# Two tiles of the slots' second MLP product made together on TensorE, the last quarter of both at the end

## The chip, the core and the metric

The kernel runs on one core of a Trainium2 chip. A core has TensorE (matrix products, PE in the profile, its weight loads PEld), VectorE (DVE), ScalarE (ACT), GpSimd (POOL) and SyncE (SP, which issues DMAs). They run side by side and wait for each other through semaphores. TensorE writes its sums into PSUM, eight banks of 128x512 fp32 numbers; ScalarE and VectorE read them there. The metric is the device time of one execution in microseconds (us), as the median of several runs. Lower is better.

## What is computed

The reference has a slot-attention block and, behind it, a routed transformer block. The change touches the first. For each of 4 samples there are 1024 keys and values and 1024 "slots" of 512 numbers, and three rounds (T = 3) refine the slots:

```python
slots = q_mu + jnp.exp(q_logsig) * noise
for _ in range(T):
    prev = slots
    q = _ln(slots, lnq_g, lnq_b) @ wq + bq
    logits = jnp.einsum('bnd,bkd->bnk', k, q) / scale
    attn = jax.nn.softmax(logits, axis=-1) + EPS_ATTN
    attn = attn / jnp.sum(attn, axis=1, keepdims=True)
    upd = jnp.einsum('bnk,bnd->bkd', attn, v)
    slots = upd @ wu + bu + prev
    h = _ln(slots, lnm_g, lnm_b) @ w1 + b1
    slots = jax.nn.gelu(h, approximate=False) @ w2 + b2 + slots
    slots = _ln(slots + x_cls[:, None, :], lnp_g, lnp_b)
```

The product with `w2` in the line before the last is the second MLP product. `w1` and `w2` are 512x512.

## The kernel before

**Tiles.** The 1024 slots of a sample are eight tiles of 128 rows, numbered 0 to 7 here as j in the code. Twelve calls of `slot_round` follow each other (4 samples, 3 rounds each). I number the calls 1 to 12 (g = 0 to 11). Calls 3, 6, 9 and 12 are the last rounds of their samples; 3, 6 and 9 prepare the next sample's slots, and call 12 leads over to the routed block. The other eight calls (1, 2, 4, 5, 7, 8, 10, 11) have one and the same order of work at the place of the change and are called the eight plain rounds.

**Precision.** Each factor is held as a high and a low half (names ending in h and l), and `mm3` (lines 219 to 221) makes one product out of three matmuls: low by high, high by low, high by high. A product over 512 rows of contraction has four quarters (C = 4), so 12 matmuls of 128x512 into one bank.

**The MLP.** `hidden(h, f)` makes quarter f of the hidden layer for half h of the slots (tiles 0 to 3 or 4 to 7) in a bank. ScalarE reads it twice as GELU (lines 1930 and 1931, into `gbuf` and the high half `gT1h`), and GpSimd subtracts the two for the low half `gT1l` (`split_gelu`, line 2619), which adds one to the semaphore `g_split`. `down(j)` multiplies tile j's columns of the four quarters with `w2` into bank `DB[j]` = (2, 3, 4, 5, 4, 5, 0, 1)[j]. So `down(4)` and `down(5)` use banks 4 and 5 again, after tiles 2 and 3; they first wait for `down_read`, which says that VectorE has read the earlier tile from the bank. Before each quarter, `down` waits for that quarter's `g_split`. At its end it adds one to `down_done`.

**VectorE behind it.** The order on each engine is fixed by hand. For each tile VectorE runs `residual(j)`: wait for `down_done`, add the bank to `slots` into `tbuf` (line 2379), and take mean and variance of it (lines 1994 and 1996); then `gained(j)` (line 2386), and, after GpSimd has made the reciprocal deviation `rs_p` (lines 2517 and 2519), `new_slots(j)` (line 2392) with the statistics of the next round's norm. ScalarE normalizes the tile (line 1744), TensorE transposes it (`z_transpose`, line 1496), ScalarE takes the transpose's high half (`zTh`, line 1762) and VectorE its low half (`z_lo(yn, j)`, line 2042, `zTl`). In a plain round VectorE's order from tile 3's new slots on is: `new_slots(3)`, `z_lo` 0 and 1, `residual(4)`, `gained(4)`, `residual(5)`, `new_slots(4)`, `gained(5)`, `z_lo` 2 and 3, `residual(6)`, `new_slots(5)`, `gained(6)`, `residual(7)`, `new_slots(6)`, `gained(7)`, `z_lo` 4, `new_slots(7)`, and, in the next call, `z_lo` 5, 6 and 7.

**TensorE around it.** Its order is `hidden(1, 0)` to `hidden(1, 3)`, transposes 0 and 1, `down(4)`, `down(5)`, transpose 2, `down(6)`, transpose 3, `down(7)`. The next call opens with `logits(0, 0)` (keys by the first four tiles of slots; waits for `z_lo` 3), transpose 4, `logits(1, 0)`, transpose 5, `logits(2, 0)`, and then `logits_pair(0, 2)`, matmuls of 128x256 that use tiles 4 and 5 and so wait for `z_lo` 5. In call 12 the place of the transposes is taken by two transposes of the routed block, `T(0, 0)` and `T(0, 1)`.

Of the kernel before, what the change touches and what calls it, by code (L numbers as in the profile page):

```python
# [5 lines left out]
C = D // P  # L6
# [13 lines left out]
AHEAD = 4  # L20
# [21 lines left out]
def build(nc, a):  # L42
# [3 lines left out]
    def sem(name):  # L46
        if name not in sems:
            sems[name] = nc.alloc_semaphore(name)
        return sems[name]

    def at(name, shape, off, dt=f32):
        return nc.alloc_sbuf_tensor_at(name, shape, dt, offset=BASE + off)

    def scratch(name, shape, dt=f32):
# [14 lines left out]
    w2 = [at("w2h", [P, C, D], 16 * KB, f32r), at("w2l", [P, C, D], 24 * KB, f32r)]  # L69
# [6 lines left out]
    gT = [[at(f"gT{h}h", [P, C, 512], OP + 16 * KB * h, f32r),  # L76
           at(f"gT{h}l", [P, C, 512], OP + 16 * KB * h + 8 * KB, f32r)] for h in range(2)]
# [136 lines left out]
    def bank(i):  # L214
        return ps[:, i, :]

    def mm3(pe, out, lhs, rhs, start, stop):
        (lh, ll), (rh, rl) = lhs, rhs
        nc.tensor.matmul(out, ll, rh, start=start, stop=False)  # L219
        nc.tensor.matmul(out, lh, rl, start=False, stop=False)  # L220
        return nc.tensor.matmul(out, lh, rh, start=False, stop=stop)  # L221

    def pair(t, *ix):
        return t[0][ix], t[1][ix]

    ALL = slice(None)

    def cut(j, n=P):
        return slice(j * n, (j + 1) * n)
# [1053 lines left out]
    with block:  # L1283
# [190 lines left out]
        def _(pe):  # L1474
# [31 lines left out]
            def z_transpose(yc, j):  # L1506
                pe.wait_ge(sem("zo_z"), yc + j + 1)
                if j >= 2:
                    pe.wait_ge(sem("lo_z"), yc + j - 1)
                transposes(zbuf[:, j % 2, :], 6 + j % 2).then_inc(sem("tr_z"), 1)  # L1510
# [86 lines left out]
            def slot_round(g, last):  # L1597
                n8 = g * NT
# [89 lines left out]
                DB = (2, 3, 4, 5, 4, 5, 0, 1)  # L1688

                def down(j):  # L1690
                    h = j // 4
                    if j in (4, 5):
                        pe.wait_ge(sem("down_read"), AHEAD + n8 + j - 1)
                    for f in range(C):
                        pe.wait_ge(sem("g_split"), g * 2 * C + h * C + f + 1)
                        last_ = mm3(pe, bank(DB[j]), pair(gT[h], ALL, f, cut(j % 4)), pair(w2, ALL, f, ALL),
                                    f == 0, f == C - 1)
                    last_.then_inc(sem("down_done"), 1)

                yn = yc + NT  # L1700
                if t == 0 and b:
# [11 lines left out]
                if g == 0:  # L1713
                    pe.wait_ge(sem("w_split"), 2)
                down(0); down(1); m_transpose(7); down(2); down(3)
                hidden(1, 0); hidden(1, 1); hidden(1, 2); hidden(1, 3)
                if not last:
                    z_transpose(yn, 0); z_transpose(yn, 1)
                down(4); down(5)
                if last:  # L1720
                    T(0, 0); T(0, 1)
                if not last:
                    z_transpose(yn, 2)
                down(6)
                if not last:
                    z_transpose(yn, 3)
                down(7)

            for g in range(B * ROUNDS):
                slot_round(g, g == B * ROUNDS - 1)  # L1730
# [1040 lines left out]
```

## Time and profile before

| | us |
|---|---|
| median of 3 runs | 2335.23 (2334.9 to 2336.6) |
| the profiled execution | 2333.35 |
| its span on the core, first to last instruction | 2331.6 |
| TensorE busy | 2293.4 (98% of the span) |
| VectorE busy | 1571.5 (67%) |
| ScalarE busy | 976.1 (42%) |
| GpSimd busy | 990.0 (42%) |

Between the profiled execution and its span lie 1.75 us, and the profiled execution is 1.9 us under the median. The matmuls of TensorE are pipelined: one that reads 0.39 us long is followed by the next 0.23 us after its start. So a gap in the stream can be longer than the idle time that the profile gives, and starts are compared here, not busy times. The chain that ended last runs through TensorE for 79% of the span, VectorE for 11% and GpSimd for 5%. Each round takes about 142 us.

### The profile page before, as it was taken

To read this page: it belongs to the slowest core of one execution; us is meant where nothing else is said; L and a number is where in the kernel's file an instruction comes from. 1 tells how busy PE (TensorE), PEld (TensorE's weight loads), DVE (VectorE), ACT (ScalarE), POOL (GpSimd) and SP (SyncE) were. 2 spreads that over 40 slices of the span, in tenths; PEclk is the share of its full clock that TensorE was granted. 3 is DMA by queue.
4 is the path that set the end of the run, shared out by engine and by line. 5 is a ranking of instruction groups with operands and counts; after the bars stand their busy time and mean duration, and the time that the engine had idled before them with its cause. 6 is when DMAs were issued, how large, how long until landed. Compare 5 with 4: busy or idle time off the path is not lost.

```text
span 2331.6 us, 30994 instructions
## 1 busy us (share of the span) xinstructions
PE 2293.4 (98%) x11509; PEld 1885.6 (81%) x11509; DVE 1571.5 (67%) x3069; ACT 976.1 (42%) x1650; POOL 990.0 (42%) x1345
## 2 busy tenths in 40 slices
PE   8999999999999999999999999999999999899998
PEld 4888888888888888888888888888888887777886
DVE  6778557757477574778757667785675868764642
ACT  2566443343333334333333433334333335766332
POOL 1576235152453525435454352464535246753200
PEclk9999999999999999999999999999999999999999
DMA  5587000000052000013400002250000012204330
GB/s 204 179 315 278 1 1 1 1 1 1 37 199 86 1 24 5 14 51 127 154 5 14 14 5 59 109 172 5 10 14 5 19 46 91 69 33 145 96 113 19
DMA packets 87126, 158.59 MB, mean 68 GB/s; under 512 B 10801, under 2 KB 33337, under 8 KB 83134
## 3 DMA queue, kind: packets, MB, share of 16 engines
q1 hardware_dynamic: 82838, 150.26, 18.8%
q0 software_dynamic: 2688, 6.31, 0.9%
q8 instruction: 92, 1.51, 0.3%
q14 instruction: 58, 0.48, 0.1%
q10 hardware_dynamic: 1450, 0.04, 0.0%
HBM read 106.21 MB, written 50.37 MB: 67 GB/s over the span
## 4 chain that ended last, share of the span: by engine, by line
PE 79%; DVE 11%; POOL 5%; issue 2%; ACT 2%; DMA 1%; ACTq 0%; SPq 0%; DVEq 0%; POOLq 0%
PE ps L219 25%; PE ps L221 24%; PE ps L220 24%; PE ps L1496 3%; DVE moments L1994 3%; POOL gT1l L2619 2%; DVE slots L2392 1%; DVE zTl L2042 1%; DVE tbuf L2379 1%; DVE tbuf L2386 1%; PE ps L1649 1%; DVE mx L2339 1%; ACT prob L1897 1%; PE ps L1481 1%; PE ps L447 1%
## 5 line engine op out<-in xcount | busy, mean ns | idle before, releaser
L219 PE MATMUL ps<-zTh,kTl 128*128 128x512 f32 (+1 forms) x912 | 332.2, 364 | 2.8 <-ACT prob L1897 2.2
L221 PE MATMUL ps<-zTh,kTh 128*128 128x512 f32 (+1 forms) x912 | 324.6, 356 | 0.0
L220 PE MATMUL ps<-zTl,kTh 128*128 128x512 f32 (+1 forms) x912 | 324.4, 356 | 0.0
L219 PE MATMUL ps<-vh,prob_lo 128*128 128x512 f32 x768 | 306.1, 399 | 0.0
L221 PE MATMUL ps<-vh,prob_hi 128*128 128x512 f32 x768 | 300.1, 391 | 0.0
L220 PE MATMUL ps<-vl,prob_hi 128*128 128x512 f32 x768 | 299.4, 390 | 0.0
L2517 POOL TENSOR_SCALAR rs_m<-mv_m 128x1 f32<-128x1 f32 x96 | 55.3, 576 | 542.3 <-DVE mv_m L1996 540.6
L2042 DVE TENSOR_TENSOR zTl<-ps,zTh 128x512 fp32r<-128x512 f32 x224 | 151.1, 682 | 193.0 <-ACT zTh L1762 193.0
L1897 ACT ACTIVATE prob<-ps,nb 128x1024 f32<-128x1024 f32 x96 | 107.2, 1117 | 252.7 <-DVE nb L2344 252.2
L1744 ACT ACTIVATE zbuf<-slots,rs_m 128x512 f32<-128x512 f32 x96 | 78.4, 817 | 303.3 <-POOL rs_m L2522 303.3
L219 PEld LDWEIGHTS ps<-zTh,kTl 128*128 128x128 f32 x912 | 172.0, 189 | 35.0 <-DVE zTl L2042 7.0
L221 PEld LDWEIGHTS ps<-zTh,kTh 128*128 128x128 f32 x912 | 172.0, 189 | 24.9
L220 PEld LDWEIGHTS ps<-zTl,kTh 128*128 128x128 f32 x912 | 172.3, 189 | 23.5
L1762 ACT ACTIVATE zTh<-ps 128x512 fp32r<-128x512 f32 x224 | 130.6, 589 | 143.7 <-PE ps L1496 143.6
L2361 DVE SCALAR_TENSOR_TENSOR slots<-ps,rcol,slots 128x512 f32<-128x512 f32 x96 | 72.0, 750 | 148.6 <-PE ps L221 147.8
L221 PEld LDWEIGHTS ps<-vh,prob_hi 128*128 128x128 f32 x768 | 144.1, 188 | 31.3
L220 PEld LDWEIGHTS ps<-vl,prob_hi 128*128 128x128 f32 x768 | 144.5, 188 | 28.2
L219 PEld LDWEIGHTS ps<-vh,prob_lo 128*128 128x128 f32 x768 | 144.4, 188 | 28.0 <-issue 0.2
L1867 ACT ACTIVATE prob_hi<-prob 128x1024 fp32r<-128x1024 f32 (+2 forms) x120 | 103.8, 884 | 126.3 <-PE ps L221 101.9
L219 PE MATMUL ps<-zTh,w1l 128*128 128x512 f32 x384 | 150.7, 392 | 0.0
L221 PE MATMUL ps<-zTh,w1h 128*128 128x512 f32 x384 | 149.7, 390 | 0.0
L220 PE MATMUL ps<-zTl,w1h 128*128 128x512 f32 x384 | 149.4, 389 | 0.0
(328 smaller groups left out, 5652.2 us busy)
## 6 DMA issues: line engine op xcount, KB each, us to landing
ctx<-in_ctx_dram SPq DMA_DIRECT2D x8, 1024.0 KB, 7.6
slots<-in_x_dram SPq DMA_DIRECT2D x8, 1024.0 KB, 6.6
kT_d<-kTh SPq DMA_DIRECT2D x6, 1024.0 KB, 8.0
kT_d<-kTl SPq DMA_DIRECT2D x6, 1024.0 KB, 10.6
s_d<-slots SPq DMA_DIRECT2D x6, 1024.0 KB, 5.1
v_d<-vh SPq DMA_DIRECT2D x6, 1024.0 KB, 8.9
v_d<-vl SPq DMA_DIRECT2D x6, 1024.0 KB, 11.7
kTh<-kT_d SPq DMA_DIRECT2D x3, 2048.0 KB, 10.5
```

Of the source, the lines that this page charges most:

```text
L219: nc.tensor.matmul(out, ll, rh, start=start, stop=False)
L220: nc.tensor.matmul(out, lh, rl, start=False, stop=False)
L221: return nc.tensor.matmul(out, lh, rh, start=False, stop=stop)
L1496: last = nc.tensor.transpose(bank(dst_bank)[:, cut(c)], src[:, cut(c)], ident[:, :])
L1744: return A.activation(out, src, ACT.Identity, bias=rs[k][:, j, 1:2], scale=rs[k][:, j, 0:1])
L1762: A.activation(zT[0][:, :, cut(col)], bank(6 + j % 2).rearrange("p (c n) -> p c n", c=C), ACT.Copy)\
L1867: A.activation(prob_hi[:, j % 2, ix, :], prob[:, j // 4, ix, cut(j % 4)], ACT.Copy)\
L1897: A.activation(prob[:, :, i, :], ps[:, b0:b0 + 2, :], ACT.Exp, bias=nb[:, i:i + 1], scale=LOGIT_SCALE, accum_out=esum[:, i:i + 1]).then_in ...
L1994: V.bn_stats(st[k][:, s, :], src).then_inc(sem(f"mv_{k}"), 1)
L2042: V.tensor_tensor(zT[1][:, :, cut(col)], bank(6 + j % 2).rearrange("p (c n) -> p c n", c=C), zT[0][:, :, cut(col)].bitcast(f32), ALU.subtr ...
L2361: V.scalar_tensor_tensor(slots[:, j, :], bank(j % 6), rcol[:, j:j + 1], slots[:, j, :], ALU.mult, ALU.add).then_inc(sem("upd_read"), 1)
L2517: G.tensor_scalar(rs[k][:, j, 1:2], mv[k][:, j, 1:2], LN_EPS, None, ALU.add).then_inc(sem(f"nm_{k}"), 1)
```

## The change

`down` keeps its form for six tiles. Tiles 4 and 5 are made by a new helper, `down_two(4)`, which writes the first three quarters of tile 4, then the first three of tile 5, then the last quarter of tile 4 and the last of tile 5. Each quarter's matmuls are now in `down_part(j, f)`, with the wait for `g_split` in front and the step of `down_done` behind the fourth. The wait for `down_read` stays in front of each tile's first quarter. No matmul is added or taken away, and the banks and all other engines' orders stay the same.

```diff
                     for f in range(C):
-                        pe.wait_ge(sem("g_split"), g * 2 * C + h * C + f + 1)
-                        last_ = mm3(pe, bank(DB[j]), pair(gT[h], ALL, f, cut(j % 4)), pair(w2, ALL, f, ALL),
-                                    f == 0, f == C - 1)
-                    last_.then_inc(sem("down_done"), 1)
+                        down_part(j, f)
+
+                def down_part(j, f):
+                    h = j // 4
+                    pe.wait_ge(sem("g_split"), g * 2 * C + h * C + f + 1)
+                    last_ = mm3(pe, bank(DB[j]), pair(gT[h], ALL, f, cut(j % 4)), pair(w2, ALL, f, ALL),
+                                f == 0, f == C - 1)
+                    if f == C - 1:
+                        last_.then_inc(sem("down_done"), 1)
+
+                def down_two(j):
+
+                    for k in range(2):
+                        pe.wait_ge(sem("down_read"), AHEAD + n8 + j + k - 1)
+                        for f in range(C - 1):
+                            down_part(j + k, f)
+                    down_part(j, C - 1); down_part(j + 1, C - 1)
...
-                down(4); down(5)
+                down_two(4)
```

TensorE, call 1, from the third quarter of `down(4)` on, before. The rows do not name the bank. The wait for `down_read` opens tile 5; the three matmuls ahead of it are tile 4's last quarter.

```order
L219 MATMUL ps<-w2h_51,gT1l_64 128x512 [waits g_split]
L220 MATMUL ps<-w2l_52,gT1h_63 128x512
L221 MATMUL ps<-w2h_51,gT1h_63 128x512
L219 MATMUL ps<-w2h_51,gT1l_64 128x512 [waits g_split]
L220 MATMUL ps<-w2l_52,gT1h_63 128x512
L221 MATMUL ps<-w2h_51,gT1h_63 128x512
L219 MATMUL ps<-w2h_51,gT1l_64 128x512 [waits g_split,down_read]
L220 MATMUL ps<-w2l_52,gT1h_63 128x512
L221 MATMUL ps<-w2h_51,gT1h_63 128x512
```

The same place after the change, from the same third quarter on. Tile 5 now opens directly behind it.

```order
L219 MATMUL ps<-w2h_51,gT1l_64 128x512 [waits g_split]
L220 MATMUL ps<-w2l_52,gT1h_63 128x512
L221 MATMUL ps<-w2h_51,gT1h_63 128x512
L219 MATMUL ps<-w2h_51,gT1l_64 128x512 [waits g_split,down_read]
L220 MATMUL ps<-w2l_52,gT1h_63 128x512
L221 MATMUL ps<-w2h_51,gT1h_63 128x512
L219 MATMUL ps<-w2h_51,gT1l_64 128x512 [waits g_split]
L220 MATMUL ps<-w2l_52,gT1h_63 128x512
```

Nine matmuls of tile 5 now stand between tile 4's third quarter and its last.

VectorE, call 1, `residual(4)`, `gained(4)`, `residual(5)` and `new_slots(4)`; this order is the same before and after.

```order
L2379 TENSOR_TENSOR tbuf_71<-ps,slots_66 128x512 [waits down_done,slots_ready,cb_added]
L1994 BN_STATS moments_88<-tbuf_71 128x6 [waits down_read]
L1996 BN_AGGR mv_p_92<-moments_88 128x2 [waits mv_p]
L2386 SCALAR_TENSOR_TENSOR tbuf_71<-tbuf_71,mv_p_92,gp_row_67 128x512 [waits mv_p]
L2379 TENSOR_TENSOR tbuf_71<-ps,slots_66 128x512 [waits down_done,slots_ready,cb_added]
L1994 BN_STATS moments_88<-tbuf_71 128x6 [waits down_read]
L1996 BN_AGGR mv_p_92<-moments_88 128x2 [waits mv_p]
L2392 SCALAR_TENSOR_TENSOR slots_66<-tbuf_71,rs_p_99,bp_row_68 128x512 [waits nm_p,gp_step]
```

The first row waits for tile 4's `down_done`, and the three behind it have to run before the fifth row, which waits for tile 5's.

## Rows read from the trace of the kernel before

**Rows 1.** Waits of the whole span: us in total, times, longest.

```profile
PE ps L219 <- POOL gT1l L2619: 2.5, 11, 0.7
DVE tbuf L2379 <- PE ps L221: 11.3, 16, 1.1
```

**Rows 2.** Timeline, PE, call 1, `down(4)` and `down(5)`: start, duration, instruction [idle before].

```profile
382.50 0.39 PE L221 MATMUL ps<-w2h,gT1h 128*128 128x512 f32 x1
383.07 0.50 PE L219 MATMUL ps<-w2h,gT1l 128*128 128x512 f32 x1 [0.19 <-POOL gT1l L2619]
...
383.64 0.39 PE L221 MATMUL ps<-w2h,gT1h 128*128 128x512 f32 x1
...
386.38 0.40 PE L221 MATMUL ps<-w2h,gT1h 128*128 128x512 f32 x1
```

**Rows 3.** Timeline, DVE, call 1, from `residual(4)` to `z_lo` 5.

```profile
384.17 0.69 DVE L2379 TENSOR_TENSOR tbuf<-ps,slots 128x512 f32<-128x512 f32 x1 [1.10 <-PE ps L221]
...
385.84 0.78 DVE L2386 SCALAR_TENSOR_TENSOR tbuf<-tbuf,mv_p,gp_row 128x512 f32<-128x512 f32 x1
386.91 0.69 DVE L2379 TENSOR_TENSOR tbuf<-ps,slots 128x512 f32<-128x512 f32 x1 [0.29 <-PE ps L221]
...
390.69 1.28 DVE L2042 TENSOR_TENSOR zTl<-ps,zTh 128x512 fp32r<-128x512 f32 x2
...
395.03 0.72 DVE L2386 SCALAR_TENSOR_TENSOR tbuf<-tbuf,mv_p,gp_row 128x512 f32<-128x512 f32 x1
395.66 0.68 DVE L2379 TENSOR_TENSOR tbuf<-ps,slots 128x512 f32<-128x512 f32 x1
...
401.65 0.66 DVE L2042 TENSOR_TENSOR zTl<-ps,zTh 128x512 fp32r<-128x512 f32 x1
```

**Rows 4.** Busy time by stretch: us, busy of PE, PEld, DVE, ACT, POOL, granted clock, DMA.

```profile
386.91:402.31 15.40, 15.39 (x75) 12.39 (x73) 14.91 (x28) 4.73 (x7) 8.86 (x18) 1.00 0.00 0
1940.00:1947.00 7.00, 6.32 (x29) 4.89 (x28) 4.34 (x6) 4.01 (x7) 5.80 (x10) 1.00 0.55 184
1968.00:1972.00 4.00, 4.00 (x26) 3.33 (x26) 3.20 (x12) 1.91 (x10) 1.55 (x5) 0.57 0.00 0
```

**Rows 5.** Timeline, PE, opening of call 2: `logits(0, 0)`, and `logits_pair(0, 2)`.

```profile
393.01 0.39 PE L219 MATMUL ps<-zTh,kTl 128*128 128x512 f32 x1
...
401.92 0.39 PE L221 MATMUL ps<-zTh,kTh 128*128 128x512 f32 x1
402.36 0.39 PE L219 MATMUL ps<-zTh,kTl 128*128 128x256 f32 x1
```

**Rows 6.** Timeline, PE, call 3, around `down(4)`'s last quarter.

```profile
666.39 0.39 PE L221 MATMUL ps<-w2h,gT1h 128*128 128x512 f32 x1
...
667.19 0.40 PE L220 MATMUL ps<-w2l,gT1h 128*128 128x512 f32 x1
```

**Rows 7.** Timeline, DVE, call 3: `residual(4)` and `z_lo` 2.

```profile
669.36 0.68 DVE L2379 TENSOR_TENSOR tbuf<-ps,slots 128x512 f32<-128x512 f32 x1
...
671.66 0.69 DVE L2042 TENSOR_TENSOR zTl<-ps,zTh 128x512 fp32r<-128x512 f32 x1 [0.67 <-ACT zTh L1762]
```

**Rows 8.** Timeline, DVE, call 6: `residual(4)` and `z_lo` 3.

```profile
1096.56 0.68 DVE L2379 TENSOR_TENSOR tbuf<-ps,slots 128x512 f32<-128x512 f32 x1
...
1101.85 0.66 DVE L2042 TENSOR_TENSOR zTl<-ps,zTh 128x512 fp32r<-128x512 f32 x1
```

**Rows 9.** Timeline, PE, call 6's end: third quarter of `down(4)`, later `logits(0, 0)`.

```profile
1091.81 0.39 PE L221 MATMUL ps<-w2h,gT1h 128*128 128x512 f32 x1
...
1102.56 0.50 PE L219 MATMUL ps<-zTh,kTl 128*128 128x512 f32 x1
```

**Rows 10.** Timeline, PE, call 12: `down(4)`, and the first scores behind the rounds.

```profile
1943.29 0.39 PE L221 MATMUL ps<-w2h,gT1h 128*128 128x512 f32 x1
1944.36 0.50 PE L219 MATMUL ps<-w2h,gT1l 128*128 128x512 f32 x1 [0.69 <-POOL gT1l L2619]
...
1967.71 0.50 PE L434 MATMUL ps<-qk 32*128 32x128 f32 x4 [2.21 <-DVE nmax L907]
```

## The prediction
> **What bounds the kernel now.** I read the chain that ended last first: TensorE has 79% of it and is busy for 98% of the span. So a stop in TensorE's stream counts in full unless the stream stops again later for something that did not move. The view of waits names the stop that the change is about: TensorE waits 11 times for GpSimd's `gT1l`, the low half of the GELU, 2.5 us in all. The same view holds a second row that matters more: VectorE waits 16 times for TensorE before line 2379, 11.3 us in all [rows 1]. Sixteen is two in each of the eight plain rounds, `residual(4)` and `residual(5)`, as the timeline of VectorE shows with 1.10 and 0.29 us [rows 3]. So VectorE takes tile 4 as soon as TensorE has it.
>
> Then the timeline, engine by engine, from `down(4)` to the next call's `logits_pair(0, 2)`. VectorE is busy for 14.91 of the 15.40 us from `residual(5)` to the end of `z_lo` 5 [rows 4], and `z_lo` 5 ends at 401.65 + 0.66 = 402.31. TensorE's last full matmul starts at 401.92 and the next should follow 0.23 later, at 402.15. It starts at 402.36, 0.05 behind the end of `z_lo` 5 [rows 5]. So over the tail of each plain round the two engines are level, and VectorE is the later one by 0.2 us. That decides the case.
>
> **What the change takes away.** The stream's step is (386.38 - 383.64) / 12 = 0.228 us [rows 2]. From the last matmul of the third quarter (382.50) to the last of the fourth (383.64) lie three matmuls, 0.68 us of work in 1.14, so the stop costs 0.46 us. With nine matmuls of tile 5 in between (9 x 0.228 = 2.05 us), the fourth quarter is asked for at 384.78 instead of 382.73. GpSimd has it by 383.07, where TensorE now starts, so 1.7 us of cover are left. The stop goes in all eight plain rounds, and the new wait for `down_read` at tile 5 finds tile 3 read long before. At the end of `down(5)` TensorE is 0.46 us ahead of today.
>
> **What the change puts off.** Tile 4's last matmul starts at 382.50 + 12 x 0.228 = 385.24 instead of 383.64. `residual(4)` starts 0.53 us behind that start (384.17 - 383.64), so at 385.77: 1.60 us later. Tile 5's last matmul comes at 385.92, so tile 5 is free to be read at 386.45. But VectorE must do tile 4 first. From `residual(4)` to `gained(4)` it takes 385.84 - 384.17 = 1.67 us without a wait. The instruction behind a `gained` can start 0.63 us (395.66 - 395.03, a short one of 0.72) to 0.78 us (the whole length of this one) after it [rows 3]. So `residual(5)` starts at 388.07 to 388.22, against 386.91: 1.16 to 1.31 us later. I take 1.2, as back-to-back rows overlap like the short one.
>
> **What hides the delay: nothing.** Behind `residual(5)` VectorE has no wait for TensorE up to `z_lo` 5, it is in arrears there. GpSimd's reciprocals follow VectorE's means and move with them. ScalarE is busy for 4.73 of the 15.40 us [rows 4]. On the way `z_lo` 3 ends at 390.69 + 1.28 + 1.2 = 393.17, while TensorE, 0.46 early, wants `logits(0, 0)` at 393.01 - 0.46 = 392.55 [rows 3, 5]. It stops there for 0.6 us, which eats the gain on the spot and leaves TensorE some 0.2 to 0.3 us behind today. The second stop is at `logits_pair(0, 2)`: `z_lo` 5 ends at 403.51 and TensorE goes on at 403.56 instead of 402.36, **1.2 us later in every plain round**. What follows (transposes 6 and 7, the softmax) starts from TensorE and VectorE at this point, so it all moves along. Eight rounds give 8 x 1.2 = +9.6 us.
>
> **The other four calls.** Call 3: the fourth quarter's first two starts show a stop of 667.19 - 666.39 - 2 x 0.228 = 0.34 us [rows 6]. `residual(4)` would start at 666.39 + 12 x 0.228 + 0.53 = 669.66 instead of 669.36, and the 0.67 us that VectorE idles ahead of `z_lo` 2 for ScalarE and TensorE take that up [rows 7]. The gain stays: -0.34. Call 6 (9 is alike): tile 4 would be ready at 1091.81 + 2.74 + 0.53 = 1095.08, before VectorE comes to it at 1096.56, so nothing is put off. But TensorE waits at `logits(0, 0)`, which starts at 1102.56, for `z_lo` 3, which ends at 1101.85 + 0.66 = 1102.51 [rows 8, 9]. Arriving earlier only makes that wait longer: 0. Call 12: a stop of 1.07 - 0.23 = 0.84 us and the restart goes [rows 10], VectorE does not wait for tile 4 there (it is none of the 16), and the next thing TensorE waits for is VectorE again, 2.21 us for `nmax`: 0.
>
> **The sum.** 9.6 - 0.34 = +9.3 us. On the profiled execution, 2333.35 us, that is 2342.6; on the median, 2335.23, it is 2344.5. The bounds of the unknown pieces: 1.16 to 1.31 per plain round give 9.3 to 10.5; up to 0.4 us of gain in each of calls 6 and 9 and 0.9 in call 12, if their waits give way, take 1.7 off. Own range of the forecast: 2342.5 to 2345.4, and with 1 us for the median's scatter 2341.5 to 2346.5.
>
> **A rule weighed.** Tile 4 is read and worked on from 384.17 to 386.62 while tile 5's matmuls run to 386.38 [rows 2, 3]; after the change that overlap is all but gone. The Trainium skill, "Perfetto Trace Analysis", Optimizing Tensor Performance, has it that independent groups of matmuls should rotate through the banks so that the reading of one overlaps the next group's matmuls. This change speaks against that; by that rule the sum is what I have. The same page, Optimization Strategy, would have one find the gaps on the engine to be filled and take away what blocks them, which by itself gives the sum of the first rival.
>
> **Rivals.**
> - **The tail has room, the gain stays.** If the delay of tile 4 is absorbed, the plain rounds give -0.46 each: -3.7, with call 3 -4.0, so 2331.2. For it: VectorE is busy for only 67% of the whole span. Against it: 14.91 of 15.40 us in the tail, and no wait in it to take up more than 0.2. It decides once `z_lo` 5 has 1.2 us to spare; it has less than nothing. If the calls 6, 9 and 12 gave their part too (0.4 + 0.4 + 0.9), 2329.5. Not slower, 0.08; faster by over 0.2% only in the second form, 0.03 of these.
> - **Half of it is absorbed.** VectorE's start times hang on small gaps and on its sharing with GpSimd (the two `gained` shown take 0.72 and 0.78 us). If such pieces give back 0.6 us a round: 8 x 0.6 - 0.3 = +4.5, 2339.7. The gaps in the tail add up to 15.40 - 14.91 = 0.49 us, and most are the distance between two dependent instructions. 0.10.
> - **The new stop lowers TensorE's clock.** The stop at `logits_pair(0, 2)` is about 1.1 us, after one of 0.6. In this trace, after the 2.21 us wait in call 12 the granted clock reads 0.57 over 4 us: most of it at the lower level, 1.2 of 2.4 GHz, 0.43 x 4 = 1.7 us of work lost. After the gap of 1.07 us there it stays at 1.00 [rows 4, 10]. The new stops are like the second. If the clock fell in every plain round: 8 x (1.2 + 1.7) - 0.3 = +22.9, 2358. The Trainium skill, "TensorE: Matmul & The Clock Gate", A second HAM failure mode, tells of a kernel whose short idles between groups brought the clock down again and again; the trace disagrees so far, as its eleven short stops leave the clock alone. 0.04.
> - **The wait moves but the stop stays.** If GpSimd's fourth quarter came later than 2.05 us after it is now asked for, the stop would remain. The longest today is 1.07 us, in call 12. It is under 0.01.
>
> **How the numbers follow.** Forecast 0.78, half absorbed 0.10, all absorbed 0.08, clock 0.04. The likeliest gives 2344.5. The range runs from 2338.5, which takes in the half-absorbed case, to 2347.5. 0.2%, about what a measurement of this kernel can tell from no change, is 4.7 us: under 2330.5 is faster, over 2339.9 slower. Faster 0.03. Same 0.13: the rest of the absorbed case and most of the half-absorbed. Slower 0.84.
>
> **What would show it.** In the changed kernel's timeline, call 1: no stop in `down(4)`; `residual(4)` 1.6 us later, its wait for TensorE 2.7 instead of 1.10 us; no wait before `residual(5)`; and the view of waits with 8 waits before line 2379 where there were 16. A wait of TensorE for `zTl` at `logits(0, 0)` in the plain rounds, and one of about 1.1 us at `logits_pair(0, 2)`. Each plain round, about 142 us now, gets 1.2 us longer. I am wrong if plain rounds get shorter, if VectorE shows a wait between `residual(5)` and `z_lo` 5, or if the granted clock is under 1.00 in the tails.

## The result

| | before | changed |
|---|---|---|
| median, us | 2335.07 (6 runs, 2334.63 to 2336.6) | 2343.72 (6 runs, 2342.12 to 2345.11) |
| span of the profiled execution, us | 2331.6 | 2341.1 |
| TensorE busy, us | 2293.4 | 2293.8 |
| VectorE busy, us | 1571.5 | 1570.1 |

The ratio of the changed kernel to the one before is 1.0036, with a 95% interval of 1.0026 to 1.0047: it is slower by 8.65 us, where 9.3 was forecast. The work is the same, as the busy times show. What grew is waiting. Of the executions behind the experiments below, one of the kernel before and one with two quarters ahead ran at a mean granted clock of 0.65 and 0.56 and took 3274 and 3836 us; the ratios leave both out, and without its one the median with two quarters ahead is 2338.27 us.

The stop that the change was made against is gone: the view of waits of the changed kernel has no row of TensorE for `gT1l` any more, which stood there with 2.5 us [rows 1]. In its place stands a wait of TensorE for VectorE, and VectorE's wait ahead of its first read of the bank (now line 2392, all lines below the change are 13 higher) has gone from 16 times and 11.3 us to this:

```profile
DVE tbuf L2392 <- PE ps L221: 21.6, 9, 2.7
PE ps L219 <- DVE zTl L2055: 12.4, 18, 0.9
```

The columns are us in total, times and the longest. Nine is one in each plain round and one in call 3. TensorE waits 18 times, two in each plain round and one in each of calls 6 and 9. Now VectorE's timeline in call 1, which answers to [rows 3]:

```profile
385.72 0.69 DVE L2392 TENSOR_TENSOR tbuf<-ps,slots 128x512 f32<-128x512 f32 x1 [2.67 <-PE ps L221]
386.45 0.69 DVE L2007 BATCH_NORM_STATS2 moments<-tbuf 128x6 f32<-128x512 f32 x1
387.18 0.18 DVE L2009 BATCH_NORM_AGGREGATE mv_p<-moments 128x2 f32<-128x6 f32 x1
387.39 0.78 DVE L2399 SCALAR_TENSOR_TENSOR tbuf<-tbuf,mv_p,gp_row 128x512 f32<-128x512 f32 x1
388.09 0.68 DVE L2392 TENSOR_TENSOR tbuf<-ps,slots 128x512 f32<-128x512 f32 x1
...
391.87 1.28 DVE L2055 TENSOR_TENSOR zTl<-ps,zTh 128x512 fp32r<-128x512 f32 x2
...
402.82 0.66 DVE L2055 TENSOR_TENSOR zTl<-ps,zTh 128x512 fp32r<-128x512 f32 x1
```

The first row is `residual(4)`: it waits 2.67 us instead of 1.10 and starts 1.55 later. The row at 388.09 is `residual(5)`, 1.18 us later than 386.91, and it has no wait: tile 5 has been ready for some time, and VectorE is still at tile 4. `z_lo` 5 in the last row is 1.17 us later than 401.65. In between nothing was made up. TensorE at the opening of call 2, which answers to [rows 5]:

```profile
393.20 0.50 PE L219 MATMUL ps<-zTh,kTl 128*128 128x512 f32 x1 [0.53 <-DVE zTl L2055]
...
403.54 0.39 PE L219 MATMUL ps<-zTh,kTl 128*128 128x256 f32 x1 [0.91 <-DVE zTl L2055]
```

These are the two new stops, at `logits(0, 0)` and at `logits_pair(0, 2)`. The second starts 1.18 us later than 402.36. The view of busy time by stretch, over the same 15.40 us of VectorE's work as [rows 4], from `residual(5)` on:

```profile
388.09:403.49 15.40, 14.02 (x67) 10.90 (x65) 14.91 (x29) 4.13 (x6) 9.23 (x18) 1.00 0.00 0
```

VectorE is busy for the same 14.91 us, and TensorE for 14.02 where it was 15.39.

A round's length can be read without the scatter of whole runs, as the distance between the first row maxima of two calls (`mx`, line 2339 before, 2352 after). In the changed kernel the first rows of calls 2 and 3 are

```profile
410.69 1.23 DVE L2352 TENSOR_REDUCE mx<-ps 128x1 f32<-128x1024 f32 x1 [1.79 <-PE ps L221]
553.80 1.23 DVE L2352 TENSOR_REDUCE mx<-ps 128x1 f32<-128x1024 f32 x1 [1.79 <-PE ps L221]
```

so the distance in which call 2's tail lies is 143.11 us; before they stand at 409.51 and 551.47, 141.96 us. The table has these lengths, named by the call whose tail lies in them, for all kernels of this study:

| kernel | plain rounds, us (8) | call 3 | calls 6, 9 |
|---|---|---|---|
| before | 141.93 to 142.02 | 141.49 | 142.26, 142.27 |
| changed | 143.11 to 143.19 | 141.15 | 142.27, 142.27 |
| one quarter ahead | 141.75 to 141.79 | 141.15 | 142.27, 142.30 |
| two quarters ahead | 142.45 to 142.56 | 141.14 | 142.30, 142.28 |
| signal held back | 143.00 to 143.41 | 141.53 | 142.30, 142.30 |
| last rounds only | 141.94 to 142.10 | 141.14 | 142.30, 142.28 |
| changed, `z_lo` 5 early | 142.05 to 142.11 | 141.17 | 142.28, 142.31 |
| before, `z_lo` 5 early | 141.61 to 141.79 | 141.53 | 142.29, 142.30 |
| one quarter, `z_lo` 5 early | 141.14 to 141.16 | 141.15 | 142.30, 142.28 |

Changed less before over the eleven distances is 9.1 us.

### The profile page after: what moved, and what is told of

The parts are those of the page before. It is cut to its first block, busy times and chain, and to the rows that moved or that the text cites. A ratio compares the mean times of both kernels' runs of the same rounds, so it can differ in the third digit from the quotient of the medians.

```text
span 2341.1 us, 30994 instructions
## 1 busy us (share of the span) xinstructions
PE 2293.8 (98%) x11509; PEld 1887.1 (81%) x11509; DVE 1570.1 (67%) x3069; ACT 976.2 (42%) x1650; POOL 989.7 (42%) x1345
## 4 chain that ended last, share of the span: by engine, by line
PE 83%; DVE 11%; POOL 2%; issue 2%; ACT 2%; DMA 0%; ACTq 0%; DVEq 0%; POOLq 0%
PE ps L219 26%; PE ps L221 25%; PE ps L220 25%; PE ps L1496 3%; DVE moments L2007 3%; DVE slots L2405 1%; DVE tbuf L2392 1%; DVE zTl L2055 1%; DVE tbuf L2399 1%; PE ps L1649 1%; PE ps L447 1%; ACT prob L1910 1%; PE ps L1481 1%; DVE mx L2352 1%; PE ps L434 0%
```

## The experiments

My theory: the loss is VectorE's. The change hands it tile 4 later than it takes tile 5 sooner, and VectorE has no room up to the value that TensorE waits for. The rival theories: the split of the sums and the turning between two banks cost TensorE time by themselves; or the new stop at `logits(0, 0)` is what costs. None of the seven kernels leaves work out.

**How many quarters of tile 5 go ahead.** In two kernels `down_two` got a number, 1 or 2, where the change has 3.

```diff
-                    for k in range(2):
-                        pe.wait_ge(sem("down_read"), AHEAD + n8 + j + k - 1)
-                        for f in range(C - 1):
-                            down_part(j + k, f)
-                    down_part(j, C - 1); down_part(j + 1, C - 1)
+                    pe.wait_ge(sem("down_read"), AHEAD + n8 + j - 1)
+                    for f in range(C - 1):
+                        down_part(j, f)
+                    pe.wait_ge(sem("down_read"), AHEAD + n8 + j)
+                    for f in range(ahead):
+                        down_part(j + 1, f)
+                    down_part(j, C - 1)
+                    for f in range(ahead, C):
+                        down_part(j + 1, f)
```

One quarter:

> The same output as before. Only one quarter of tile 5 (three matmuls, 0.68 us) is put between tile 4's third quarter and its last. VectorE's tail theory: the stop of 0.46 us goes, since the last quarter is asked for at 382.73 + 0.68 = 383.41, behind 383.07. Tile 4 is ready 0.23 us later than before the change, so residual(5) starts at 384.40 + 2.37 = 386.77 against 386.91, and logits_pair(0, 2) of the next call 0.14 us earlier. Eight plain rounds: -1.1 us, call 3: -0.34, together -1.5 us, about 2333.6. Theory that the split itself or the turning between two banks costs TensorE 1.2 us a round: the time stays near that of the change, +9 us. Theory that TensorE's stop at logits(0, 0) is what costs: no such stop here, so -4 us, the whole stop gained.

Measured: 2333.34 us against 2335.64, ratio 0.9996 (0.9987 to 1.0005), not to be told from no change by the whole runs. The rounds are clearer: 141.77 us on average, 0.19 less than before, against 0.14 expected; with call 3 that is 8 x 0.19 + 0.34 = 1.9 us. The stop has gone as in the change, though the sums are split and the banks take turns as there, so neither costs anything. What TensorE won is spent at `logits_pair(0, 2)` (timeline of TensorE):

```profile
402.18 0.39 PE L221 MATMUL ps<-zTh,kTh 128*128 128x512 f32 x1
402.93 0.38 PE L219 MATMUL ps<-zTh,kTl 128*128 128x256 f32 x1 [0.36 <-DVE zTl L2059]
```

The distance of 0.75 us should be 0.23. There is no stop at `logits(0, 0)` here, and still TensorE got back only 0.19 of 0.46 us. So that stop is not what takes the gain here.

Two quarters:

> The same output as before. Two quarters of tile 5 are put between tile 4's third quarter and its last. VectorE's tail theory: tile 4 is read 0.91 us later than before the change, residual(5) at 385.08 + 2.37 = 387.45, 0.54 us later, and so is logits_pair(0, 2). Eight plain rounds +4.3, call 3 -0.34: +4.0 us, about 2339.1. Theory that the split itself costs: as the change, +9 us. The three runs with one, two and three quarters should lie on a line with 0.68 us for each quarter and plain round, 5.5 us for each quarter in all.

Measured: 2338.81 us, ratio 1.0015 (1.0006 to 1.0025), and 142.47 us a plain round, +0.51 against +0.54 expected. One, two and three quarters give -0.19, +0.51 and +1.18 us: steps of 0.70 and 0.67 for the 0.68 us that three matmuls take. Every 0.68 us by which tile 4 comes later lengthens the round by all of it.

**The delay without the split.** TensorE's matmuls stay in the order of before; VectorE alone is held back.

```diff
                     for f in range(C):
...
+                        if j == 5 and f == 1 and t < ROUNDS - 1:
+                            last_.then_inc(sem("tile5_half"), 1)
                     last_.then_inc(sem("down_done"), 1)
...
+                    if j == 4 and t < ROUNDS - 1:
+                        dve.wait_ge(sem("tile5_half"), b * (ROUNDS - 1) + t + 1)
                     dve.wait_ge(sem("down_done"), n8 + j + 1)
```

> The same output as before. TensorE's order is that of the kernel before, nothing is interleaved, and its stop of 0.46 us stays. Only VectorE is held back: in the eight plain rounds residual(4) also waits for the second quarter of tile 5. VectorE's tail theory: residual(4) starts at 385.01 + 0.53 = 385.54 instead of 384.17, residual(5) at 387.91, 1.00 us later, logits_pair(0, 2) 1.0 us later; eight rounds +8.0 us, about 2343.1. Theory that the interleaved matmuls or banks are the cost: no change, 2335.

Measured: 2344.3 us (four runs, 2339.6 to 2346.3), ratio 1.0045 (1.0030 to 1.0061), and 1.13 us more in a plain round on average, where 1.0 was expected (one call has 1.45). The rows of VectorE and then TensorE in call 1 and at the opening of call 2:

```profile
382.30 0.69 DVE L2383 TENSOR_TENSOR tbuf<-ps,slots 128x512 f32<-128x512 f32 x1 [2.61 <-PE ps L221]
...
384.67 0.68 DVE L2383 TENSOR_TENSOR tbuf<-ps,slots 128x512 f32<-128x512 f32 x1
```

```profile
379.12 0.39 PE L221 MATMUL ps<-w2h,gT1h 128*128 128x512 f32 x1
379.73 0.50 PE L219 MATMUL ps<-w2h,gT1l 128*128 128x512 f32 x1 [0.23 <-POOL gT1l L2623]
...
400.11 0.39 PE L219 MATMUL ps<-zTh,kTl 128*128 128x256 f32 x1 [0.91 <-DVE zTl L2044]
```

The stop for `gT1l` is still there (0.61 us from start to start), nothing is interleaved, and the loss of the change appears all the same, with the same wait of 0.91 us for `z_lo` 5. From `residual(4)` to `residual(5)` it is 384.67 - 382.30 = 2.37 us, as in the changed kernel (388.09 - 385.72). This shows the cause by itself: the moment at which VectorE may take tile 4.

**The other calls.** `down_two` in calls 3, 6, 9 and 12 only.

```diff
-                down_two(4)
+                if t == ROUNDS - 1:
+                    down_two(4)
+                else:
+                    down(4); down(5)
```

> The same output as before. The change is made in calls 3, 6, 9 and 12 alone; the eight plain rounds have the order of before. VectorE's tail theory: call 3 is 0.34 us shorter, calls 6 and 9 do not move since TensorE waits there for z_lo 3, call 12 does not move: -0.3 us, 2334.8. Theory that every stop taken away is gained: -0.34 - 0.43 - 0.43 - 0.9 = -2.1 us. Theory that the split itself costs 1.2 us a call: +4.8 us.

Measured: 2334.74 against 2335.64 us, ratio 1.0000 (0.9991 to 1.0010). Call 3 is 0.35 us shorter, 6 and 9 are not. Behind call 6 TensorE arrives earlier and waits:

```profile
1102.31 0.50 PE L219 MATMUL ps<-zTh,kTl 128*128 128x512 f32 x1 [0.57 <-DVE zTl L2058]
```

The kernel before has no idle time printed at this place [rows 9], but its matmul too starts 0.48 us behind the one ahead of it, 0.25 more than a step: a stop that the matmuls' overlap hides from the column of idle time.

**Room for VectorE.** In a plain round `z_lo` 5, for which TensorE waits, runs behind `new_slots(7)` and its statistics, 1.6 us, for which TensorE does not wait yet. The edit swaps them:

```diff
-                for j in range(4 if g == 0 else 6 if t == 0 else 5, NT):
+                for j in range(4 if g == 0 else 6, NT):
...
-                z_lo(yn, 4)
+                z_lo(yn, 4); z_lo(yn, 5)
                 new_slots(7)
```

With the change:

> The same output as before. The changed kernel, with one more edit on VectorE in the eight plain rounds: z_lo 5 of the next round runs ahead of new_slots(7) instead of behind it, which gives the value that TensorE waits for 1.6 us of room. VectorE's tail theory: z_lo 5 is done at about 401.9, before TensorE wants it at 402.47, so the stop at logits_pair(0, 2) goes and with it 1.1 us a round; the stop at logits(0, 0) for z_lo 3 stays and eats the gain of 0.46 us. A plain round takes 142.0 us as before the change instead of 143.1; with call 3's -0.34 about 2335. Theory that the loss is in TensorE's own stream: 143.1 a round stays, 2344.

Measured: 2337.03 against 2335.58 us, ratio 1.0006 (0.9997 to 1.0015); 142.07 us a plain round against 142.0 expected. TensorE's rows at `logits_pair(0, 2)`:

```profile
401.24 0.39 PE L221 MATMUL ps<-zTh,kTh 128*128 128x512 f32 x1
401.47 0.28 PE L219 MATMUL ps<-zTh,kTl 128*128 128x256 f32 x1
```

The step is 0.23, so the stop is gone, and with it 1.07 of the 1.18 us that the change lost. `down_two` is as in the change. Compared with the kernel before that has the same edit (next, 141.67 us), the change still costs 0.40 us a plain round. The stop at `logits(0, 0)` is still there:

```profile
392.21 0.50 PE L219 MATMUL ps<-zTh,kTl 128*128 128x512 f32 x1 [0.53 <-DVE zTl L2055]
```

So once `z_lo` 5 is in time, this first stop has a price of its own; it too is tile 4's delay, arriving through `z_lo` 3. 0.32 us of the 0.40 can be read here (the stop costs 0.78, less the 0.46 gained); the rest was not traced.

On the kernel before:

> The same output as before. The kernel before with the same edit on VectorE alone (z_lo 5 ahead of new_slots(7) in the eight plain rounds). TensorE's gap ahead of logits_pair(0, 2) is 0.21 us and costs 0.1 more in the second matmul: 0.31 us a round, 141.65 instead of 141.96, together -2.5 us, 2333. If tile 7, whose new slots come 0.6 us later, becomes what TensorE waits for at transpose 7 (zbuf ready at 404.6, wanted at 405.5), the gain is smaller.

Measured: 2331.29 us, ratio 0.9984 (0.9975 to 0.9993), 141.67 us a plain round on average, 0.29 less where 0.31 was expected: 8 x 0.29 = 2.3 us. The ratio says 3.7, with an interval from 1.6 to 5.8.

With one quarter ahead:

> The same output as before. One quarter of tile 5 ahead of tile 4's last quarter, and z_lo 5 ahead of new_slots(7). VectorE's tail theory: the stop of 0.46 us is gone, tile 4 only 0.2 us later, no stop at logits(0, 0), and z_lo 5 in time (401.9 against 402.4), so TensorE runs through: 141.96 - 0.46 - 0.31 = 141.2 us a plain round, 8 x -0.77 = -6.1, call 3 -0.34, together -6.5 us, about 2329. If both edits take from the same gap, only -2.5 us as with the second alone.

Measured: 2330.44 us, ratio 0.9975 (0.9966 to 0.9985), and 141.15 us a plain round, 0.81 less than before. The two edits together give more than the sum of what each gives alone (0.19 and 0.29 make 0.48, together 0.81), because each takes away a stop that ate part of the other's gain. 8 x 0.81 + 0.34 = 6.8 us by the rounds, 5.8 by the ratio (3.5 to 7.9). This kernel is faster than the one before and the changed one. TensorE's rows at the same place show the step of 0.22:

```profile
402.26 0.39 PE L221 MATMUL ps<-zTh,kTh 128*128 128x512 f32 x1
402.48 0.28 PE L219 MATMUL ps<-zTh,kTl 128*128 128x256 f32 x1
```

## Why the prediction was right

- **The stop goes.** Right: 0.46 us in a plain round, with cover to spare. Tile 4's last quarter runs without a gap in the changed kernel.
- **Tile 4 comes 1.6 us later.** Forecast for `residual(4)` 385.77, measured 385.72.
- **Tile 5 has to wait for VectorE.** `residual(5)` was put between 388.07 and 388.22, and stands at 388.09. The delay is 1.18 us; 1.2 was taken.
- **Nothing hides it.** `logits_pair(0, 2)` was forecast for 403.56 and starts at 403.54. The experiment with the held signal shows that this delay alone makes the loss, and the three doses (one, two and three quarters ahead) that all of it arrives. The rival of the half-absorbed delay asked for 0.6 us a round; nothing was absorbed.
- **The stop at `logits(0, 0)`.** Forecast 0.6 us. From the last matmul ahead of it (392.29) to the second in it (393.54) the trace of the changed kernel has 0.79 us more than two steps: the first starts 0.68 late, and the step behind it is 0.34 instead of 0.23. Less the 0.46 gained, TensorE is 0.32 us behind, where 0.2 to 0.3 was forecast. In the changed kernel this costs nothing on top, since the second stop would only be longer without it; without the second stop it does cost (0.40 us a round, above).
- **Call 3 gains 0.34.** Right: 141.49 to 141.15. VectorE waits 0.20 us for tile 4 there and takes it back ahead of `z_lo` 2. This is the ninth wait ahead of line 2392, where the prediction named eight.
- **Calls 6 and 9: 0.** Right, 142.26 to 142.27 and 142.27 to 142.27.
- **Call 12: 0, with one wait overlooked.** TensorE gets the 0.84 us and waits them away in two places, of which the prediction named only the second:

```profile
1970.46 0.50 PE L434 MATMUL ps<-qk 32*128 32x128 f32 x4 [0.72 <-DVE tbuf L2392]
1976.79 0.50 PE L434 MATMUL ps<-qk 32*128 32x128 f32 x4 [2.33 <-DVE nmax L907]
```

  The second wait was 2.21 us [rows 10]. Its matmul starts 138.47 us behind the call's first `mx`, where it was 138.46, at a granted clock of 1.00 up to there in both. To the end of the span it is 502.8 us against 502.4, by one execution each.
- **The wait for `down_read`.** I wrote of the plain rounds that it finds tile 3 read long before, and there it does. Of call 12 I said nothing, and there VectorE reads tile 3 only just in time:

```profile
1951.80 0.68 DVE L2392 TENSOR_TENSOR tbuf<-ps,slots 128x512 f32<-128x512 f32 x1
```

```profile
1952.36 0.39 PE L221 MATMUL ps<-w2h,gT1h 128*128 128x512 f32 x1
1952.58 0.45 PE L219 MATMUL ps<-w2h,gT1l 128*128 128x512 f32 x1
1952.87 0.39 PE L220 MATMUL ps<-w2l,gT1h 128*128 128x512 f32 x1
```

The read ends at 1952.48, and tile 5's first matmul starts at 1952.58; the step behind it is 0.29 instead of 0.23. If that is this wait, it is 0.06 us, and the waits above take it up.

- **The sum.** +9.3 forecast, 9.1 by the rounds, 8.65 by the medians. The clock did not fall: it is 1.00 in the tail shown above, with its two new stops, and over the calls 1 to 11 (1.00 from 260 to 1838 us of the trace), and every plain round has the same length. So the rival of the clock is out. The Trainium skill's rule of "Perfetto Trace Analysis", Optimizing Tensor Performance, that independent groups of matmuls should rotate through the banks so that one's reading overlaps the next, told this case rightly: the three doses trade away that overlap step by step.

## What to carry to other kernels

Two sums that are finished together reach their reader together, and a reader that works on one at a time gets the first late and the second no sooner. Before filling a stop with the next tile's work, look at what the engine behind it does from there to the next wait of the bottleneck: if it has no idle time, each microsecond by which its first input is late is lost, and each by which the bottleneck is early is waited away. Fill the stop with as little as covers it (here one quarter instead of three), and first move work that nobody waits for behind the value that is waited for; the two together made this kernel 5.8 us faster than before.

## What the runs showed of the hardware

Turning between two half-made sums in two banks cost TensorE nothing that can be seen: in call 1 of the changed kernel 20 steps through `down_two`, from 381.34 to 385.88, take 0.227 us each, over all three turns. After a stop the first step was longer, 0.34 us instead of 0.23 (393.20 to 393.54).

Whole runs scatter by some us (2329.9 to 2339.2 in 26 runs of the kernel before), although a kernel's plain rounds agree within 0.2 us but for one call with the signal held back. A part of it is TensorE's clock behind the rounds. In the stretch of 23 us that begins 138.7 us behind call 12's first `mx`, the granted clock was 0.93 before, 0.78 in the profiled execution with one quarter ahead and 1.00 in that of the change:

```profile
1968.00:1991.00 23.00, 22.94 (x166) 18.26 (x165) 19.96 (x68) 18.52 (x64) 15.76 (x22) 0.93 0.02 2
```

```profile
1967.00:1990.00 23.00, 22.94 (x140) 17.63 (x139) 16.47 (x63) 15.99 (x53) 12.98 (x20) 0.78 0.01 1
```

```profile
1977.00:2000.00 23.00, 22.94 (x178) 18.44 (x177) 21.16 (x78) 19.95 (x66) 16.42 (x24) 1.00 0.01 2
```

In all three TensorE had waited 2.2 to 2.3 us for `nmax` just before. In the second the granted clock is 0.50 from 1970 to 1974, the lower of its two levels, 1.2 of 2.4 GHz. In its 23 us TensorE started 140 matmuls where the third stretch has 178, and the part from call 12's first `mx` to the end took 507.5 us against 502.4 before and 502.8 in the change, whose own fall came later (0.77 from 2025 to 2035). That is why the profiled span with one quarter ahead reads 2335.7 us, more than before, while each of its rounds is shorter. What decides in which execution the clock falls there is left open; for gains of 2 us the rounds' lengths are the better measure.
